# First FFN of a macaron block on one core: weight subtractions and remainders exchanged between VectorE and GpSimd, and the last four roots in two pairs

## What is computed

```python
x = x + 0.5 * _L0_ffn_ref(_layernorm(x, axis=-1), ...)
x = x + _L0_attn_ref(_layernorm(x, axis=-1), ...)
x = x + 0.5 * _L0_ffn_ref(_layernorm(x, axis=-1), ...)

def _quantized_matmul(x, w, scale):
    wq = w.astype(jnp.float8_e4m3fn).astype(x.dtype)
    return jnp.einsum('bsi,io->bso', x, wq) * scale
...
gate = jax.nn.silu(_quantized_matmul(x, gate_w, gate_scale))
up = _quantized_matmul(x, up_w, up_scale)
return _quantized_matmul(gate * up, down_w, down_scale)
```

## Time and profile before

| what | value |
|---|---|
| median of 3 runs | 159.17 us (159.16 to 159.94) |
| the profiled execution | 159.67 us, of which its span in the profile is 157.3 us |
| TensorE busy | 151.1 us, 96% of the span |
| VectorE busy | 124.5 us, 79% |
| ScalarE busy | 77.8 us, 49% |
| GpSimd busy | 68.4 us, 43% |
| granted TensorE clock | 1.00 throughout |

### The profile page before, as it was taken

How to read it: one execution, slowest core, us unless ns; L and a number is a source line. 1 busy time by engine, 2 the same in 40 slices (tenths; PEclk the granted TensorE clock), 3 DMA queues, 4 the chain that set the end, 5 groups by cost and what they waited for, 6 DMA issues and landing times.

```text
span 157.3 us, 3410 instructions
## 1 busy us (share of the span) xinstructions
PE 151.1 (96%) x1199; PEld 117.4 (75%) x1199; DVE 124.5 (79%) x271; ACT 77.8 (49%) x179; POOL 68.4 (43%) x76
## 2 busy tenths in 40 slices
PE   5998999999999999999999999999999999999992
PEld 2375688788979568957786878668688887888991
DVE  0897999998897769579696969896944999656684
ACT  3476997687113150615435272637565648473310
POOL 3446344774973400183655647186699420000000
PEclk9999999999999999999999999999999999999999
DMA  4999402804000000000000000000000000001103
GB/s 125 328 368 307 158 0 76 328 5 133 0 0 4 0 0 4 0 0 0 6 0 4 2 4 0 4 0 2 4 2 0 0 4 0 0 0 63 38 33 133
DMA packets 7007, 8.40 MB, mean 53 GB/s; under 512 B 448, under 2 KB 5712, under 8 KB 6992
## 3 DMA queue, kind: packets, MB, share of 16 engines
q1 hardware_dynamic: 6816, 8.13, 15.4%
q10 hardware_dynamic: 176, 0.07, 0.3%
HBM read 7.15 MB, written 1.05 MB: 52 GB/s over the span
## 4 chain that ended last, share of the span: by engine, by line
PE 61%; POOL 13%; DVE 10%; issue 9%; DMA 2%; ACT 1%; POOLq 0%; DVEq 0%; ACTq 0%
PE bank L1157 26%; PE bank L1185 13%; POOL grstd L338 7%; PE bank L1213 5%; PE bank L1283 3%; DVE sc L798 3%; PE bank L1338 2%; DMA xt<-in_L_attn_x 2%; PE bank L1259 2%; DVE stats L694 2%; POOL rstd L316 2%; POOL state L346 2%; PE bank L1227 2%; PE bank L1230 2%; POOL ve L314 1%
## 5 line engine op out<-in xcount | busy, mean ns | idle before, releaser
L1157 PE MATMUL bank<-hh,up_r 128*128 128x512 f32 x92 | 25.5, 400 | 0.1
L1157 PE MATMUL bank<-hh,gate_r 128*128 128x512 f32 x92 | 25.6, 401 | 0.0
L1185 PE MATMUL bank<-down_r,fhi 128*128 128x256 f32 x96 | 24.1, 289 | 0.0
L338 POOL TENSOR_TENSOR grstd<-gve,neg_half 128x16 f32<-128x16 f32 x8 | 23.5, 2932 | 0.7
L1185 PE MATMUL bank<-down_r,flo 128*128 128x256 f32 x96 | 23.4, 282 | 0.0
L453 ACT ACTIVATE gact<-bank,vec 128x512 f32<-128x512 f32 x24 | 16.3, 685 | 9.1 <-PE bank L1157 8.3
L798 DVE TENSOR_TENSOR sc<-bank,msk 128x512 f32<-128x512 f32 x32 | 20.6, 680 | 0.0
L1157 PEld LDWEIGHTS bank<-hh,up_r 128*128 128x128 f32 x92 | 16.8, 188 | 4.3 <-issue 0.5
L461 ACT ACTIVATE fhi<-fuse 128x512 fp32r<-128x512 f32 x24 | 14.6, 625 | 10.8 <-DVE fuse L741 10.8
L1157 PEld LDWEIGHTS bank<-hh,gate_r 128*128 128x128 f32 x92 | 16.9, 188 | 4.0 <-ACT gate_r L402 0.4
L1185 PEld LDWEIGHTS bank<-down_r,fhi 128*128 128x128 f32 x96 | 18.1, 188 | 0.7 <-issue 0.2
(11 more groups left out here) (90 smaller groups left out, 284.5 us busy)
## 6 DMA issues: line engine op xcount, KB each, us to landing
raw<-in_rotation SPq DMA_DIRECT2D x1, 1536.0 KB, 7.8
out<-xt SPq DMA_DIRECT2D x8, 128.0 KB, 1.7
raw<-in_L_ffn_down_w SPq DMA_DIRECT2D x2, 384.0 KB, 7.3
wqkv<-in_L_attn_w_qkv SPq DMA_DIRECT2D x1, 768.0 KB, 9.6
xt<-in_L_attn_x SPq DMA_DIRECT2D x2, 256.0 KB, 3.6
xt<-in_L_attn_x SPq DMA_DIRECT2D x1, 512.0 KB, 5.4
raw<-in_rotation SPq DMA_DIRECT2D x1, 512.0 KB, 3.4
raw<-in_L_ffn_gate_w SPq DMA_DIRECT2D x1, 384.0 KB, 6.0
```

Of the source, the lines that this page charges most:

```text
L338: pool.tensor_tensor(grstd[:, c % 2], gve[:, :], neg_half[:, :], ALU.pow).then_inc(grstd_done, 1)
L1157: mm = pe.matmul(dst[:, :], wr[m][:, k * I + i * P:k * I + (i + 1) * P], half[:, k, g % NG, :], start=(k == 0 and half is hhi), stop=(k == ...
L1185: mm = pe.matmul(downs[d][:, 0:C], half[:, g % NG, i, t * P:(t + 1) * P], wr["down"][:, i * C:(i + 1) * C], start=(i == 0 and half is fhi) ...
```

## The change

The subtractions of pieces 4 to 7 go from POOL to DVE, each right behind the `grid_add` of its piece. The remainders 0, 1, 5, 7 and 8 go from DVE to POOL, so that POOL has 0, 1, 3, 4, 5, 7, 8, 9 (in this order, with nothing between) and 10. The group of roots of tiles 4 to 7 becomes two groups of two, with a `shift_rows` for each. On DVE the statistics of tile 6 come ahead of the aggregation of tile 4, and `grid_step(4)` moves from before `grid_add(3)` to behind `fuse_up(0)`. PE's and ACT's lists stay as they are.

```diff
-X_ROOTS = 3
+X_ROOTS = 4
...
-SUB_ON_POOL = [1, 2, 4, 5, 6, 7]
+SUB_ON_POOL = [1, 2]
...
-REST_ON_POOL = [3, 4, 9, 10]
+REST_ON_POOL = [0, 1, 3, 4, 5, 7, 8, 9, 10]
...
-        root_groups = ([(0, 2), (2, TH), (TH, NT)] + [(n, n + 1) for n in range(NT, 2 * NT)]
+        root_groups = ([(0, 2), (2, TH), (TH, TH + 2), (TH + 2, NT)] + [(n, n + 1) for n in range(NT, 2 * NT)]
...
             roots(2)
-            subtract(4)
-            subtract(5)
-            rest_f(3)
-            subtract(6)
-            rest_f(4)
-            subtract(7)
-            rest_f(9)
+            roots(3)
+            for j in REST_ON_POOL[:-1]:
+                rest_f(j)
             add_down(0)
...
             grid_step(3)
             tile_stats(4)
             tile_stats(5)
+            tile_stats(6)
             mean_var(4)
-            tile_stats(6)
+            mean_var(5)
             tile_stats(7)
-            mean_var(5)
             mean_var(6)
             mean_var(7)
             grid_clip(3)
-            grid_step(4)
             grid_add(3)
             shift_rows(2)
             subtract(3)
+            shift_rows(3)
             fuse_up(0)
+            grid_step(4)
             grid_clip(4)
             grid_step(5)
             grid_add(4)
+            subtract(4)
             rest_h(1, 0)
             rest_h(1, 1)
             fuse_up(1)
             grid_clip(5)
             fuse_up(2)
             grid_add(5)
-            rest_f(0)
+            subtract(5)
             fuse_up(3)
             fuse_up(4)
             grid_step(6)
-            rest_f(1)
             grid_clip(6)
             rest_f(2)
             fuse_up(5)
             grid_add(6)
+            subtract(6)
             grid_step(7)
             fuse_up(6)
             fuse_up(7)
             grid_clip(7)
             grid_add(7)
-            rest_f(5)
+            subtract(7)
             fuse_up(8)
             fuse_up(9)
             rest_f(6)
-            rest_f(7)
-            rest_f(8)
             fuse_up(10)
             scale_down(0)
             scale_down(1)
```

## The result

The changed kernel takes 163.8 us (median of 4 runs, 163.73 to 165.29); the kernel before took 159.37 us beside it. The ratio is 1.0293, with a 95% interval of 1.0237 to 1.0348: slower by 4.4 us. The forecast was 162.0 with a range to 163.7, so the direction was right and the loss larger than the range allowed, by 0.1 us. The span of the profiled execution grew from 157.3 to 161.4 us.

What follows compares the result with a forecast made beforehand. TensorE bounds from 17.70 us, with VectorE nearly full. `fuse_up(8)` moves by 0.6 (`rest_h`) + 3.1 (blocking) - 0.9 = 2.8 us; 159.67 + 2.8 = 162.5, less 0.5 for the median: 162.0 us, range 158.9 to 163.7.

Steps and rivals of the forecast that it cites:

- Part 1: Roots of tiles 4 to 7 in pairs: TensorE begins `gate_up(1, up)` at 16.8 instead of 17.70 us, 0.9 us gained.
- Part 2: VectorE from `fuse_up(0)` to `rest_h`: list takes 5.3 us against 4.0, ending at 20.2; VectorE 0.6 us behind.
- wait on the operation before: VectorE steps needing the preceding operation's result: each such place costs 0.11 us.
- Part 3: VectorE from `rest_h` to `fuse_up(8)`: 13.3 us of work plus 3.1 of blocking; `fuse_up(8)` at 36.6, 2.8 us later.
- Remainder 4 fits under `fuse_up(6)` and `(7)`: 0: GpSimd's remainder 4 runs beside two VectorE operations that read PSUM, so it blocks VectorE for 0 us.
- TensorE takes it at once: `gate_up(10, up)` starts at 34.71: TensorE follows `fuse_up(8)` within 0.15 us, so its 2.8 us delay passes to TensorE there and stays.
- rival 4: Each GpSimd remainder gets in behind the one running VectorE operation; all five collide, about 4.3 us blocking: 163.2 us, chance 0.12.
- rival 1: VectorE never limits TensorE; the 0.9 us earlier start survives to the end: 158.3 us, chance 0.10.
- Rival 2: Even, within 0.5%: blocking of 0.1 to 1.7 us with early roots, up to 1.1 with middle ones; 159.2 us, chance 0.13.
- rival 3: GpSimd blocks VectorE in proportion to its work, about 1.5 to 2.2 us from `rest_h` to `fuse_up(8)`: 160.7 us, chance 0.18.
- the lower sum of 161.3: Forecast if a VectorE wait on the operation before costs nothing, as the skill page says: 0.7 us less.

Runs made afterwards that it cites:

- e5_roots_rest4: Kernel before with roots of tiles 4 to 7 in two pairs and remainder 4 on VectorE in place of GpSimd: 160.3 us, ratio 1.0060.
- e1_roots_alone: Kernel before with only the roots in pairs, statistics reordered and piece 4's mask behind `fuse_up(0)`; subtractions and remainders as before: 159.11 us, ratio 0.9982.
- e3_no_reads: Changed kernel with each remainder on GpSimd replaced by a fill of its tile with zeros, which reads no SBUF: 159.97 us, ratio 1.0039.
- e8_subs_alone: Changed kernel with remainders 0, 1, 5, 7 and 8 back on VectorE, the four subtractions staying moved: 164.09 us, ratio 1.0283.
- e6_half_reads: Changed kernel with each GpSimd remainder made a zero fill of half the columns and a subtraction of the other half: 160.87 us, ratio 1.0094.

## Why the prediction was wrong

**Part 1** was right in kind. The first pair of roots ended at 13.33 us and the second at 15.11, the late end of the 14.2 to 15.1 that stood there: the sum of piece 3 held up the addition (0.58 us in place of 0.22) and the subtraction of piece 3 the root (1.14 in place of 0.72). TensorE began at 17.00, 16.8 forecast, with loads that had landed 0.1 us later.

**Part 2** was right in kind and short by 0.4 us: `rest_h` ended at 20.60 (20.2 forecast), because `fuse_up(0)` began at 15.27, just outside the 14.3 to 15.1 taken. The list itself took 5.3 us, as summed. The 0.11 us for each wait on the operation before held: the subtraction of piece 4 starts 0.04 us after the sum's end at 18.41, and `rest_h`, which does not wait for it, 0.09 before the subtraction's end at 19.41.

**Part 3** holds the steps that failed, and there are two: "Remainder 4 fits under `fuse_up(6)` and `(7)`: 0", and "TensorE takes it at once: `gate_up(10, up)` starts at 34.71". I summed VectorE's delay up to `fuse_up(8)` and handed it to TensorE there. `fuse_up(8)` was indeed only 3.6 us late (37.39 against 33.82), but TensorE had long been delayed by `fuse_up(6)`, 4.5 us late. Behind that stand 4.5 us of TensorE's own work up to `gate_up(10, up)`, so that it never waited for `fuse_up(8)`, and what VectorE made up in between was worth nothing. A sum to `fuse_up(6)` has these terms: `rest_h` 1.0 us late; two subtractions more (1.7), two remainders less (1.2), three waits on the operation before (0.3); blocks of 3.5 in place of 0.7. Together 4.6 us against 4.5 measured. Of these 4.5, 4.1 are left after the down projections, where the kernel before had waits of some tenths of its own.

The place alone would not have spoiled the number. With the forecast's own terms, `rest_h` 0.6 us late and blocks of 2.1 (remainders 0, 1 and 3), the sum to `fuse_up(6)` is 2.8 us, the same as to `fuse_up(8)`. What set the two apart was remainder 4: its block, 1.08 us on mask 7, lay ahead of `fuse_up(6)`, where the forecast had nothing, while the 1.0 us that it gave remainder 5 lay behind.

In time, 162.0 became 163.8. Of these 1.8 us, `rest_h` is 0.4, the blocks are 0.4 (3.5 for 3.1), and the handover is 0.5 (4.1 us lost on TensorE, 3.6 at `fuse_up(8)`). The last 0.5 were taken off because the median of the kernel before lay under its profiled execution; the median of the changed kernel, 163.80, does not lie under its own, 163.73.

The blocks had nearly the right size in sum, but that is partly luck. Remainders 0, 1 and 3 cost 0.86, 0.43 and 1.11 us where 0.7, 0.4 and 1.0 stood; remainder 4 cost 1.08 where 0 stood and remainder 5 nothing where 1.0 stood. Remainder 4 came while the subtraction of piece 6 ran (31.67, inside 31.19 to 32.15) and went in ahead of mask 7, which had been counted as following back to back; remainder 5 then ran behind mask 7, mostly under `fuse_up(6)` and `(7)`. There rival 4 was right: a waiting GpSimd operation did get in behind the one operation that ran, as "SBUF — State Buffer" of the Trainium skill, section "Who interferes with whom", leads one to expect. Remainder 3 did the same during the clip of piece 6, and the subtraction of piece 7 in `e5_roots_rest4` during remainder 4. Why the addition at 12.63 of the earlier trace rows stayed out behind two VectorE operations is left open.

**The rivals.** The earlier start of TensorE never reached the end (`e1_roots_alone`), so rival 1 had no ground even without collisions: `e3_no_reads` is still 0.6 us slower than before. Rival 2 needed at most 1.7 us of blocking, and there were 3.5. Blocking in proportion (rival 3) is contradicted by the changed kernel itself: before, some 8 us of GpSimd work in this stretch blocked 1.9 us; now five remainders, 6.5 us by their own length, blocked 3.5. Rival 4, 163.2 us, comes nearest in time, but its 4.3 us of blocking were not there: remainder 5 hit nothing.

**The wait on the operation before.** That it costs nothing, as the Trainium skill has it ("VectorE: DVE Perf Modes", section "The DRAIN you can't avoid"), had been set against 0.11 us for each such wait. The changed kernel's rows show the cost again (0.04 us after the end with a wait, 0.09 before it without), and the lower sum of 161.3 was further off. That section of the Trainium skill adds that an operation that is not held starts earlier; with this sentence it agrees with the rows.

## What to carry to other kernels

When a list of one engine gets longer, sum its delay at each place where the bound engine waits for it, and take the worst place that is not made up by the bound engine's own work behind it; the last one is not enough. Price a move from VectorE to GpSimd by the VectorE operations that it will meet: a remainder of 0.60 us on VectorE cost it up to 1.1 us when GpSimd did it beside masks, clips, sums and remainders, and nothing where it lay beside `fuse_up`, which reads PSUM. Taking one collision away moves the next one, so a move has to be followed through both lists to the next wait.

## What was not expected of the hardware

A wait of TensorE of 2.0 to 2.2 us was in some executions followed by its lower clock (0.58 and 0.56 in two stretches of 2 us, 0.71 and 0.50 in `e8_subs_alone`) and in others not: the changed kernel's profiled execution waited 1.96 us at clock 1.00, and one of its four timed executions, the one of 165.29 us, has 0.99. By the spans it cost 1.1 to 1.7 us where it happened, and with matmuls of zeros in the wait it did not happen. What decides it was not tried.

A fill on GpSimd inside a VectorE remainder, which reads two SBUF tensors, cost neither anything (0.53 us for the fill at 26.52 of `e3_no_reads`, 0.69 for the remainder). Beside a clip it did: the clip took 0.62 us in place of 0.55, and in `e6_half_reads` the fill at 26.62, beside the clip of piece 6, took 0.60 us in place of 0.31.
